# A three-layer graph network on one core: the order of the first seventy microseconds

## The chip, the cores and the metric

The kernel runs on one core of a Trainium2 chip. Its time is what one execution takes on the device, in microseconds; several executions are timed and their median is given. One more execution is recorded by the hardware profiler, and all rows of a trace come from that one.

Each core has TensorE (matmuls and transposes), VectorE (in the trace DVE), ScalarE (ACT), GpSimd (POOL) and SyncE (SP, which here only issues transfers). Every engine works off its own list in order, and the lists are tied by semaphores.

## The reference

```python
edge_index = stack([src, dst])                  # 20000 edges, 1250 nodes, 512 features, fp32
h = maximum(layernorm(x), 0)                    # first norm, with relu
x = x + L0(h, edge_index, ...)
h = maximum(layernorm(x), 0)
x = x + L1(h, src, dst, ...)                    # three graph convolutions

# L0 (GATv2 attention and a feed-forward net)
h1 = layer_norm(h, ln1_g, ln1_b)                # second norm
xl, xr = h1 @ Wl, h1 @ Wr                       # 8 heads of 64
e = sum over c of leaky_relu(xl[src] + xr[dst], 0.2) * att
alpha = softmax of e over the edges of one dst
h = h + segment_sum(alpha * xl[src], dst) + gat_bias
h = h + gelu(layer_norm(h, ln2_g, ln2_b) @ W1 + b1) @ W2 + b2
# L1: three times layer_norm, * 1/sqrt(out_degree), @ W[i], sum over edges, * 1/sqrt(in_degree), relu
```

## The kernel before

The 1250 nodes are ten blocks of 128 rows (NB = 10, the last one short). For the norms the blocks go in five groups of two (NG2 = 5, TWO = 2). `x_in` holds the rows as loaded and later the twice normed ones, `state` the once normed ones.

**What the first stage does.** Four things run side by side up to some 220 us.

*The norms.* For a group g, VectorE takes the statistics of the rows of x (`x_average(0, g)`: one bn_stats per block, L1340, and one bn_aggr, L1343), ScalarE the root (`x_root(0, g)`, L957), VectorE the reciprocal and the shift (`x_rows_scale(0, g)`, L1349 and L1351), and ScalarE writes the normed rows with relu to `state` (`x_norm(0, g)`, L964). The same four steps follow for the second norm, with nth = 1: VectorE reads `state` for its statistics, and ScalarE writes `x_in` (L966). The order is a pipeline over t: `norm_x(first, end)` on VectorE does average(0, t), rows_scale(0, t−1), average(1, t−2), rows_scale(1, t−3), and ScalarE's loop from L972 does root(0, t), norm(0, t−1), root(1, t−2), norm(1, t−3).

*The projections* of the twice normed rows by Wl, Wr and the folded attention weights. TensorE and ScalarE each have a generator, `projections()` (L609 and L922), cut into the same 90 steps: one for the transposes of block 0, then nine per block (the transposes of the next block, four matmuls for Wl, four for Wr with the attention product behind the last; the last block has eight). `advance(projecting, n)` runs n of them. On ScalarE a step is mostly empty: the first of a block moves the turned rows out of PSUM (`evict_block`, L913), the fifth copies the left rows (L942, to a tile), the last one the right rows (L942, to `xr_lo`) and three small things. TensorE may not write a block's right (or left) rows into their bank before ScalarE has copied those of the block before (`rows_kept`, L627). An fp32 matmul shows as two instructions in the trace.

*The sort of the edges by target*, in two radix passes on VectorE: `count_digits` compares (L1246) and scans (L1248), TensorE sums the counts (`digit_sums`), `start_digits` reads them (L1259), `place_edges` makes each edge's place (L1270, L1272 and the halving adds L1278, the first of them on 16 x 160 elements). Then `hot_batches` writes one-hot rows in batches (L1312 to L1322), and TensorE's `pick` multiplies them (L650, 32 instructions per batch, nine batches). The first pass is radix LOW = 32, the second HIGH = 40.

*The folds*: `fold_weights` multiplies Wl and then Wr by the attention vector (L1358) and sums per head (L1360). It needs the weights and the vector in SBUF.

**Where the lists meet.** TensorE advances 24 steps (COUNT_STEPS), does `digit_sums(LOW)`, advances 24 (LOW_STEPS), does pick(0), advances 18 (HIGH_STEPS), `digit_sums(HIGH)`, the other 24, and pick(1). On ScalarE the five x_norm(1, g) are followed by 6, 18, 3, 3 and 0 steps (NORM_STEPS), and then comes the rest. On VectorE: the digits of the edges (to L1411), norm_x(0, 4), the two att operations (L1414, L1416), both folds, norm_x(4, 5), count_digits(LOW), norm_x(5, 8), start_digits, place_edges(LOW), the hot batches. SyncE issues edges, x of groups 0 to 3, the zeros for two scatter tables, five rows of vectors, att, Wl, x of group 4, Wr and two biases, in this order (L437 to L459).

Behind this stage come the gathers of 352 tiles of source rows by GpSimd with the attention scores (to some 600 us), the feed-forward net, and the three convolutions. The change leaves them as they are; they start when the second pass has given the source of every edge.

Of the kernel before, what the change touches and what calls it, by code (L numbers as in the profile page):

```python
# [52 lines left out]
def build(nc, ins, out):  # L53
# [43 lines left out]
    with ExitStack() as ctx:  # L97
# [128 lines left out]
        pick_col = [rings.take(BATCH // QUARTET, max(NC, EJ), QUARTET, dt=FP16) for _ in range(2)]  # L226
        products = [ranked[:, side * KC * D:(side + 1) * KC * D] for side in range(2)]
# [112 lines left out]
        NORM_STEPS = [6, 18, 3, 3, 0]  # L340
        COUNT_STEPS, LOW_STEPS, HIGH_STEPS = 24, 24, 18
# [56 lines left out]
        x_averaged, x_rooted, x_scaled = ([count(f"{name}_{nth}") for nth in ("first", "second")] for name in ("x_averaged", "x_rooted", "x_scaled"))  # L398
# [37 lines left out]
        def sync(s):  # L436
# [7 lines left out]
            for t in range(NG2 - 1):  # L444
                load_x(t)
# [3 lines left out]
            for name, at, n in vector_rows:  # L449
                src = ins[name]  # L450
                if len(src.shape) == 2:
                    src = src.rearrange("l d -> (l d)")
                s.dma_start(columns_in[at:at + n, :], src.rearrange("(k p) -> k p", p=P)).then_inc(d_vectors, 16)
            s.dma_start(att_linear, spread(ins["L0_gnn_att"].rearrange("h c -> (h c)"))).then_inc(d_wide, 16)
            s.dma_start(w_left, w_view(ins["L0_gnn_Wl"])).then_inc(d_w[0], 16)
            load_x(NG2 - 1)
            s.dma_start(w_right, w_view(ins["L0_gnn_Wr"])).then_inc(d_w[1], 16)
# [445 lines left out]
        def scalar(a):  # L903
# [68 lines left out]
            for t in range(NG2 + 3):  # L972
                if t < NG2:
                    x_root(0, t)
                if 0 <= t - 1 < NG2:
                    x_norm(0, t - 1)
                if 0 <= t - 2 < NG2:
                    x_root(1, t - 2)
                if 0 <= t - 3 < NG2:
                    x_norm(1, t - 3)  # L980
                    if t == 3:
                        a.wait_ge(vectors_turned.sem, 1)
                        a.activation(columns[:, :], bank[:, 7, 0:VECTORS], ACT.Copy).then_inc(*columns_ready.up())
                        a.wait_ge(*columns_ready.now())
                    advance(projecting, NORM_STEPS[t - 3])
# [233 lines left out]
        def vector(v):  # L1219
# [20 lines left out]

            def count_digits(radix):

                s3 = by_digit(running, radix)
                v.wait_ge((digits_high if radix == HIGH else digits_low).sem, 1)
                v.wait_ge(*vo.now())
                v.tensor_tensor(by_digit(match, radix), over(digit[R0, :], 1, radix), digits[R0, 0:radix, :], ALU.is_equal).then_inc(*vo.up())  # L1246
# [14 lines left out]
            def place_edges(radix, by):  # L1261
# [7 lines left out]
                else:  # L1269
                    v.tensor_tensor(r3, by_digit(running, radix), over(base_of[R0, 0:radix], 2, EJ), ALU.add).then_inc(*vo.up())  # L1270
                    v.wait_ge(*vo.now())
                    v.tensor_tensor(r3, r3, by_digit(match, radix), ALU.mult).then_inc(*vo.up())  # L1272
                n = radix
                while n > 1:
# [3 lines left out]
                    v.tensor_tensor(out_ap, r3[:, 0:half, :], r3[:, n - half:n, :], ALU.add).then_inc(*vo.up())  # L1278
                    n -= half
# [54 lines left out]
            def x_average(nth, g):  # L1334
                for b in range(g * TWO, (g + 1) * TWO):
                    if nth:
                        v.wait_ge(once_normed.sem, b + 1)
                    elif b % TWO == 0:
                        v.wait_ge(d_x[g], 32)
                    v.bn_stats(stat[:, b, :], (state if nth else x_in)[:, b, :]).then_inc(*vo.up())  # L1340
                v.wait_ge(*vo.now())
                for b in range(g * TWO, (g + 1) * TWO):
                    ins_ = v.bn_aggr(x_moments[:, nth, b, :], stat[:, b, :])  # L1343
                ins_.then_inc(*x_averaged[nth].up())

            def x_rows_scale(nth, g):
# [4 lines left out]
                v.scalar_tensor_tensor(x_shift[:, nth, blocks], x_moments[:, nth, blocks, 0], -1.0, x_scale[:, nth, blocks], ALU.mult, ALU.mult).then_inc(*x_scaled[nth].up())  # L1351
# [9 lines left out]

            def norm_x(first, end):

                for t in range(first, end):
                    if t < NG2:
                        x_average(0, t)
                    if 0 <= t - 1 < NG2:
# [521 lines left out]
```

## Time and profile before

| | us |
|---|---|
| median of 3 runs | 1290.12 |
| lowest, highest | 1282.86, 1291.03 |
| the profiled execution | 1294.07 |
| its span in the trace | 1291.8 |
| busy in the span: TensorE, VectorE, ScalarE, GpSimd | 1075.5, 1029.4, 676.3, 444.2 |

The shares of busy time (TensorE 83%, VectorE 80%) are means over stages with different limits. What an edit in the first stage is worth can only be read there: which engine's list ends a wait last, and at what time the next stage can start. In the rows, a time in square brackets behind an instruction is the idle time of its engine just before it and what ended that. Groups of equal instructions are merged into one row, with "x" and their number; the second column is then the time of them all.

### The profile page before, as it was taken

The numbers are of one execution on the slowest core, as the hardware profiler recorded it, in microseconds if no ns is written. First come the engines' busy times: TensorE is split into PE (matmuls) and PEld (weight loads), VectorE is DVE, ScalarE is ACT, GpSimd is POOL, SyncE is SP. The second block draws the span as 40 slices with busy tenths as digits, with TensorE's granted clock in tenths as the row PEclk, the third lists the DMA queues.
The fourth block names the chain that finished last, engine by engine and source line by source line (L and its number), as shares of the span: only waits on it lengthen the run. The fifth ranks groups of instructions, "written<-read, shape, count | busy, mean of one in ns | idle before, by whom it ended". The sixth has DMA issues, their size and how long they took to land.

```text
span 1291.8 us, 15548 instructions
## 1 busy us (share of the span) xinstructions
PE 1075.5 (83%) x4827; PEld 800.3 (62%) x4847; DVE 1029.4 (80%) x1458; ACT 676.3 (52%) x1257; POOL 444.2 (34%) x412
## 2 busy tenths in 40 slices
PE   3979988565565656289999999699999999999998
PEld 2578456354454545145555555399888888889896
DVE  8999998587777778899999999875776778583934
ACT  4601300365555556278888888767655674342420
POOL 2071072655656555267778665000002100000000
PEclk9989889667767677589999999899999999999999
DMA  5000001655656556256666677400001202001002
GB/s 185 34 10 14 25 10 27 190 160 158 174 153 174 155 158 145 68 159 190 184 195 191 191 197 177 145 2 17 9 1 34 64 3 78 4 1 41 1 1 81
DMA packets 43434, 122.81 MB, mean 95 GB/s; under 512 B 7839, under 2 KB 8627, under 8 KB 43353
## 3 DMA queue, kind: packets, MB, share of 16 engines
q0 software_dynamic: 29184, 93.81, 27.1%
q1 hardware_dynamic: 14168, 27.98, 6.5%
q8 instruction: 44, 0.72, 0.2%
q14 instruction: 38, 0.30, 0.1%
HBM read 116.13 MB, written 5.59 MB: 94 GB/s over the span
## 4 chain that ended last, share of the span: by engine, by line
PE 56%; DVE 16%; ACT 13%; issue 7%; another core or an unknown queue 6%; DMA 1%; SPq 1%; ACTq 1%; DVEq 0%
PE bank L847 10%; PE bank L807 8%; PE bank L793 8%; PE bank L755 7%; PE bank L863 7%; PE bank L650 5%; PE bank L766 5%; PE bank L701 3%; ACT bank L1006 3%; ACT counts L1033 2%; ACT arena L991 2%; ACT hot_t L996 2%; ACT hot L920 1%; DVE counts L1248 1%
## 5 line engine op out<-in xcount | busy, mean ns | idle before, releaser
L568 POOL DMA_INDIRECT arena<-left_table,arena x352 | 364.7, 1036 | 241.1 <-issue 104.5
L701 PE MATMUL bank<-xr_hi,hot_t 128*128 x176 | 103.1, 586 | 120.6 <-ACT bank L1006 85.7
L755 PE MATMUL bank<-arena,hot 128*128 128x512 f32 x352 | 177.4, 620 | 4.0 <-DVE den_parts L1583 4.0
L1493 DVE SCALAR_TENSOR_TENSOR arena<-bank,arena 128x1024 f32<-128x1024 f32 x88 | 107.7, 1224 | 72.8 <-remote 37.0
L847 PE MATMUL bank<-counts_r,ns 128*128 128x512 f32 (+2 forms) x720 | 137.1, 349 | 0.0
L847 PEld LDWEIGHTS bank<-counts_r,ns 128*128 128x128 f32 x720 | 125.6, 188 | 10.4
L1033 ACT ACTIVATE counts<-bank 128x1280 f32 x88 | 108.9, 1237 | 39.9 <-issue 20.2
L701 PEld LDWEIGHTS bank<-xr_hi,hot_t 128*128 128x128 f32 x176 | 46.4, 264 | 130.8 <-issue 124.6
L991 ACT ACTIVATE arena<-bank,minus_own 128x512 f32<-128x512 f32 x44 | 30.2, 687 | 171.8 <-PE bank L691 86.3
L766 PE MATMUL bank<-arena 128*128 128x512 bf16 (+1 forms) x508 | 109.4, 347 | 6.6 <-DVE arena L1591 3.9
L1495 DVE TENSOR_REDUCE arena<-arena 128x16 f32<-128x1024 f32 x88 | 107.4, 1220 | 3.0
L1579 DVE TENSOR_TENSOR arena<-arena 128x1024 f32<-128x1024 f32 x88 | 107.1, 1217 | 0.0
L560 POOL DMA_INDIRECT moved<-counts x32 | 57.6, 1801 | 131.2 <-DVE counts L1297 61.7
L756 PE MATMUL bank<-den_parts,hot 128*128 128x18 f32 x176 | 101.9, 579 | 0.0
L650 PE MATMUL bank<-arena 125*125 125x160 f16 (+1 forms) x576 | 89.8, 332 | 13.1 <-DVE arena L1316 13.1
L650 PEld LDWEIGHTS bank<-arena 125*125 125x125 f16 (+1 forms) x576 | 74.8, 157 | 28.3 <-DVE arena L1316 16.6
L1006 ACT ACTIVATE bank<-arena 128x1024 f32<-128x1024 f32 x88 | 89.6, 1019 | 4.1 <-PE bank L717 2.7
L701 PE MATMUL bank<-xr_lo,hot_t 128*128 x176 | 91.0, 517 | 0.0
L1591 DVE TENSOR_SCALAR arena<-arena 128x1280 bf16<-128x1280 f16 x176 | 90.1, 553 | 0.8 <-PE bank L766 0.5
L766 PEld LDWEIGHTS bank<-arena 128*128 128x128 bf16 x528 | 52.5, 117 | 58.7 <-issue 16.7
L592 POOL CAST counts_r<-counts 128x1280 fp32r<-128x1280 f32 x10 | 13.1, 1313 | 203.9 <-issue 172.4
L629 PE MATMUL bank<-arena 128*128 128x512 f32 x160 | 77.7, 639 | 0.8 <-ACT arena L913 0.8
(248 smaller groups left out, 2203.0 us busy)
## 6 DMA issues: line engine op xcount, KB each, us to landing
arena<-left_table,arena POOLq DMA_INDIRECT x352
arena<-in_x_dram SPq DMA_DIRECT2D x18, 256.0 KB, 4.7
arena<-in_L_gnn_W_dram SPq DMA_DIRECT2D x8, 512.0 KB
arena<-in_L_gnn_W_dram SPq DMA_DIRECT2D x2, 1536.0 KB, 10.7
arena<-in_L_gnn_W_dram SPq DMA_DIRECT2D x3, 1024.0 KB, 5.4
left_table<-arena SPq DMA_DIRECT2D x10, 260.0 KB, 2.0
out_dram<-state SPq DMA_DIRECT2D x9, 256.0 KB
arena<-in_L_gnn_Wl_dram SPq DMA_DIRECT2D x1, 1024.0 KB, 9.9
```

The source lines that it names most:

```text
L568: g.indirect_dma_start(out=gathered[n % DEPTH][:, i, :], out_offset=None, in_=left_table, in_offset=bass.IndirectOffsetOnAxis(ap=src_of[:, ...
L650: ins_ = t.matmul(bank[0:out_rows, psum, 0:width], rows[R0, at[0], 0:out_rows, at[1]], pick_col[n % 2][R0, at[0], 0:width, at[1]], start=( ...
L701: ins_ = t.matmul(bank[:, 2 * (n % ZRING) + i, :], mine, part[:, bass.ds(at, 1), :].rearrange("p b n -> p (b n)"), start=False, stop=(part ...
L755: t.matmul(bank[:, psum, :], as_float(hot[c % 4]), w[:, i, :], start=(i == 0), stop=(i == 1))
L766: ins_ = t.matmul(flat[:, COUNT_AT + at:COUNT_AT + end], low_hot[n // 2 % 2][:, :, c % QUARTET], code_hot[c % 4][:, at:end], start=(c == 0 ...
L793: ins_ = t.matmul(bank[:, s, 0:cols], a[:, k, :], b[:, k, 0:cols], start=(i == 0), stop=(i == len(terms) - 1))
L847: ins_ = t.matmul(bank[:, SUM_BANKS[part][k], 0:n], lhs, rhs, start=(s == 0 and half == 0), stop=(s == NB - 1 and half == 1))
L1006: a.activation(bank[:, at:at + 2, :], gathered[n % DEPTH][:, :, 0:D], ACT.Copy).then_inc(*seeded.up())
L1033: a.activation(counts[:, :, bass.ds(at * P, P)], flat[:, COUNT_AT:COUNT_AT + NP].rearrange("p (b n) -> p b n", n=P), ACT.Copy).then_inc(*c ...
L1493: v.scalar_tensor_tensor(y, bank[:, at:at + 2, :], 0.0, over(att_relu, 1, 2), ALU.max, ALU.mult).then_inc(*rows_weighted.up())
L1495: v.tensor_reduce(sc, y.rearrange("p i (h c) -> p (i h) c", c=C), AX.X, ALU.add).then_inc(*pair_scored.up())
L1579: v.tensor_tensor(w.rearrange("p i (h c) -> p i h c", c=C), gathered[s][:, :, 0:D].rearrange("p i (h c) -> p i h c", c=C), over(weights[:, ...
```

## The change

1. **Second statistics.** VectorE's bn_stats and bn_aggr on `state` go. ScalarE's first norm (Relu) now also gives its sum over the row (`accum_out`), VectorE turns that into minus the mean (`x_mean`), and ScalarE makes a Square of the once normed rows with that as bias, whose sum is 512 times the variance (`x_spread`, results thrown away in `squares`). The root scales by 1/512.
2. **Order of the norms.** Both engines get a list written out by hand. On ScalarE the steps of the projections stand between the norms of single groups.
3. **VectorE.** The att operations come before the norms. `count_digits` is split: the comparison (`match_digits`) comes earlier. The folds stand between the steps of the first groups. The last steps of groups 3 and 4 stand inside `place_edges(LOW)`: behind its add, its multiplication and its first halving add.
4. **TensorE** advances 22, 24 and 20 steps in place of 24, 24 and 18.
5. **Loads.** SyncE issues x of groups 0 and 1, Wl, Wr, x of groups 2 to 4, and then the zeros. ScalarE's own queue issues att and the five rows of vectors, ahead of everything else it does.

```diff
+        squares = [ranked[:, LOW * EJ + i * D:LOW * EJ + (i + 1) * D] for i in range(TWO)]
...
-        NORM_STEPS = [6, 18, 3, 3, 0]
-        COUNT_STEPS, LOW_STEPS, HIGH_STEPS = 24, 24, 18
+        COUNT_STEPS, LOW_STEPS, HIGH_STEPS = 22, 24, 20
...
-            for t in range(NG2 - 1):
+            load_x(0)
+            load_x(1)
+            s.dma_start(w_left, w_view(ins["L0_gnn_Wl"])).then_inc(d_w[0], 16)
+            s.dma_start(w_right, w_view(ins["L0_gnn_Wr"])).then_inc(d_w[1], 16)
+            for t in range(2, NG2):
                 load_x(t)
...
             def x_root(nth, g):
                 blocks = slice(g * TWO, (g + 1) * TWO)
-                a.wait_ge(x_averaged[nth].sem, g + 1)
-                a.activation(x_scale[:, nth, blocks], x_moments[:, nth, blocks, 1], ACT.Sqrt, bias=eps[:, :]).then_inc(*x_rooted[nth].up())
+                if nth:
+                    a.wait_ge(x_squared.sem, (g + 1) * TWO)
+                else:
+                    a.wait_ge(x_averaged.sem, g + 1)
+                a.activation(x_scale[:, nth, blocks], x_moments[:, nth, blocks, 1], ACT.Sqrt, bias=eps[:, :], scale=1.0 / D if nth else 1.0).then_inc(*x_rooted[nth].up())
+
+            def x_spread(g):
+
+                a.wait_ge(x_centred.sem, g + 1)
+                if g:
+                    a.wait_ge(x_squared.sem, g * TWO)
+                for b in range(g * TWO, (g + 1) * TWO):
+                    a.activation(squares[b % TWO], state[:, b, :], ACT.Square, bias=x_moments[:, 1, b, 0:1], accum_out=x_moments[:, 1, b, 1:2]).then_inc(*x_squared.up())
...
-                        a.activation(state[:, b, :], x_in[:, b, :], ACT.Relu, bias=shift, scale=scale).then_inc(*once_normed.up())
+                        a.activation(state[:, b, :], x_in[:, b, :], ACT.Relu, bias=shift, scale=scale, accum_out=x_moments[:, 1, b, 0:1]).then_inc(*once_normed.up())
...
+            a.dma_start(att_linear, spread(ins["L0_gnn_att"].rearrange("h c -> (h c)"))).then_inc(d_wide, 16)
+            for name, at, n in vector_rows:
+                a.dma_start(columns_in[at:at + n, :], ins[name].rearrange("(k p) -> k p", p=P)).then_inc(d_vectors, 16)
...
+            x_root(0, 0)
+            x_norm(0, 0)
+            x_root(0, 1)
+            x_spread(0)
+            x_root(1, 0)
+            a.wait_ge(vectors_turned.sem, 1)
+            a.activation(columns[:, :], bank[:, 7, 0:VECTORS], ACT.Copy).then_inc(*columns_ready.up())
+            a.wait_ge(*columns_ready.now())
+            x_norm(1, 0)
+            advance(projecting, 1)
+            x_norm(0, 1)
+            advance(projecting, 1)
+            x_spread(1)
+            x_root(1, 1)
+            x_norm(1, 1)
+            advance(projecting, 4)
+            x_root(0, 2)
+            advance(projecting, 3)
+            x_norm(0, 2)
+            advance(projecting, 9)
+            x_spread(2)
+            x_root(1, 2)
+            x_root(0, 3)
+            x_norm(1, 2)
+            x_norm(0, 3)
+            advance(projecting, 4)
+            x_root(0, 4)
+            x_spread(3)
+            x_root(1, 3)
+            x_norm(0, 4)
+            advance(projecting, 5)
+            x_norm(1, 3)
+            x_spread(4)
+            x_root(1, 4)
+            x_norm(1, 4)
             advance(projecting, STEPS)
...
                     v.tensor_tensor(r3, by_digit(running, radix), over(base_of[R0, 0:radix], 2, EJ), ALU.add).then_inc(*vo.up())
+                    beside[0]()
                     v.wait_ge(*vo.now())
                     v.tensor_tensor(r3, r3, by_digit(match, radix), ALU.mult).then_inc(*vo.up())
+                    beside[1]()
...
                     v.tensor_tensor(out_ap, r3[:, 0:half, :], r3[:, n - half:n, :], ALU.add).then_inc(*vo.up())
+                    if n == radix and beside:
+                        beside[2]()
...
+            def x_mean(g):
+
+                own = x_moments[:, 1, g * TWO:(g + 1) * TWO, 0]
+                v.wait_ge(once_normed.sem, (g + 1) * TWO)
+                v.tensor_scalar(own, own, -1.0 / D, None, ALU.mult).then_inc(*x_centred.up())
...
-            norm_x(0, 4)
             v.wait_ge(d_wide, 16)
             v.tensor_scalar(att_relu, att_linear, 1.0 - SLOPE, None, ALU.mult).then_inc(*vo.up())
             v.wait_ge(*vo.now())
             v.tensor_scalar(att_linear, att_linear, SLOPE, None, ALU.mult).then_inc(*att_split.up())
+            x_average(0)
+            x_rows_scale(0, 0)
+            x_average(1)
+            x_mean(0)
+            x_rows_scale(0, 1)
+            match_digits(LOW)
+            x_rows_scale(1, 0)
             fold_weights(0, w_left)
+            x_mean(1)
             fold_weights(1, w_right)
-            norm_x(4, 5)
+            x_rows_scale(1, 1)
+            x_average(2)
+            x_rows_scale(0, 2)
             count_digits(LOW)
-            norm_x(5, NG2 + 3)
+            x_mean(2)
+            x_average(3)
+            x_rows_scale(1, 2)
+            x_rows_scale(0, 3)
+            x_average(4)
             start_digits(LOW).then_inc(*vo.up())
-            place_edges(LOW, EJ)
+            place_edges(LOW, EJ, {0: lambda: (x_mean(3), x_rows_scale(0, 4)), 1: lambda: x_rows_scale(1, 3), 2: lambda: (x_mean(4), x_rows_scale(1, 4))})
```

## Rows read from the trace of the kernel before

**Rows 1.** Chain of waits from the start: start us, us, what.

```profile
8.93 9.93 DMA arena<-in_L_gnn_Wl_dram
...
61.66 2.84 DVE arena L1278
```

**Rows 2.** Stages: busy us (instructions) per engine, PEclk granted clock, DMA share, GB/s.

```profile
4.00:8.00 4.00, 0.00 (x0) 0.00 (x0) 2.88 (x9) 0.30 (x1) 3.84 (x10) 1.00 0.94 285
...
51.00:69.00 18.00, 17.57 (x62) 9.09 (x60) 17.66 (x13) 11.24 (x31) 0.00 (x0) 1.00 0.10 37
...
139.00:142.00 3.00, 3.00 (x6) 1.45 (x6) 2.29 (x12) 0.00 (x0) 0.00 (x0) 0.50 0.03 8
```

**Rows 3.** VectorE in order of time: start us, us, line, operation, shapes, count.

```profile
7.67 1.29 DVE L1340 BATCH_NORM_STATS2 stat<-arena 128x6 f32<-128x512 f32 x2 [0.64 <-DMA arena<-in_x_dram]
...
11.13 1.28 DVE L1340 BATCH_NORM_STATS2 stat<-state 128x6 f32<-128x512 f32 x2
...
12.60 1.25 DVE L1340 BATCH_NORM_STATS2 stat<-arena 128x6 f32<-128x512 f32 x2
...
18.88 2.30 DVE L1358 TENSOR_TENSOR arena<-arena 128x2048 f32<-128x2048 f32 x1 [1.98 <-DMA arena<-in_L_gnn_Wl_dram]
...
47.62 1.40 DVE L1340 BATCH_NORM_STATS2 stat<-state 128x6 f32<-128x512 f32 x2
...
49.21 0.13 DVE L1349 RECIPROCAL counts<-counts 128x2 f32<-128x2 f32 x1
...
50.11 0.17 DVE L1349 RECIPROCAL counts<-counts 128x2 f32<-128x2 f32 x1 [0.56 <-ACT counts L957]
...
68.87 1.19 DVE L1312 TENSOR_TENSOR arena<-counts 125x2000 f16<-125x2000 f16 x1
```

**Rows 4.** ScalarE in order of time, the same columns.

```profile
0.80 1.28 ACT L970 ACT_TABLE_LOAD   x1 [0.80 <-PEq L1879]
...
7.07 0.30 ACT L957 ACTIVATE counts<-counts,eps 128x2 f32<-128x2 f32 x1 [4.77 <-DVE counts L1343]
...
49.97 1.51 ACT L966 ACTIVATE arena<-state,counts 128x512 f32<-128x512 f32 x2
51.38 0.58 ACT L942 ACTIVATE xr_lo<-bank 128x512 f32<-128x512 f32 x1
```

**Rows 5.** TensorE in order of time, the same columns.

```profile
33.27 8.27 PE L629 MATMUL bank<-arena 128*128 128x512 f32 x16
...
50.77 0.64 PE L606 MATMUL bank<-ident,arena 128*128 128x128 f32 x4
51.25 7.03 PE L629 MATMUL bank<-arena 128*128 128x512 f32 x16
58.12 0.96 PE L639 MATMUL bank<-arena 128*128 128x16 f32 x8
58.92 0.64 PE L606 MATMUL bank<-ident,arena 128*128 128x128 f32 x4
...
74.87 5.42 PE L650 MATMUL bank<-arena 125*125 125x160 f16 x35 [6.30 <-DVE arena L1316]
...
118.36 6.19 PE L629 MATMUL bank<-arena 128*128 128x512 f32 x14
...
137.68 0.41 PE L657 MATMUL bank<-counts,ones 125*125 125x40 f32 x2 [2.84 <-DVE counts L1254]
...
139.15 9.14 PE L629 MATMUL bank<-arena 128*128 128x512 f32 x14
```

**Rows 6.** ScalarE's groups by line: busy us, mean ns of one | idle before.

```profile
L991 ACT ACTIVATE arena<-bank,minus_own 128x512 f32<-128x512 f32 x44 | 30.2, 687 | 171.8 <-PE bank L691 86.3 <-remote 75.5 <-issue 10.0
...
L970 ACT ACTIVATE deviation<-eps 128x1 f32<-128x1 f32 x1 | 0.2, 203 | 0.0
```

**Rows 7.** Transfers by line: KB each, median us from issue to landing.

```profile
arena<-in_x_dram SPq DMA_DIRECT2D x18, 256.0 KB, 4.7
...
arena<-in_L_gnn_Wl_dram SPq DMA_DIRECT2D x1, 1024.0 KB, 9.9
```

More of the change, by code:

```diff
@@ L396, in build @@
         hot_once, hot_src, batch_hot, picked = count("hot_once"), count("hot_src"), count("batch_hot"), count("picked")
-        x_averaged, x_rooted, x_scaled = ([count(f"{name}_{nth}") for nth in ("first", "second")] for name in ("x_averaged", "x_rooted", "x_scaled"))
+        x_rooted, x_scaled = ([count(f"{name}_{nth}") for nth in ("first", "second")] for name in ("x_rooted", "x_scaled"))
+        x_averaged, x_centred, x_squared = count("x_averaged"), count("x_centred"), count("x_squared")
         once_normed = count("once_normed")
@@ L448, in sync @@
                 s.dma_start(table.rearrange("(p c) w -> p (c w)", p=n), back[0:n, 0:table.shape[0] // n, :].rearrange("p c w -> p (c w)")).then_inc(d_zeros, 16)
[L449 to L457, printed above, removed]
             s.dma_start(gat_bias, spread(ins["L0_gnn_gat_bias"])).then_inc(d_bias, 16)
@@ L971, in scalar @@
             projecting = projections()
[L972 to L985, printed above, removed]
+            x_root(0, 0)
[33 more added lines that the diff above has]
+            x_norm(1, 4)
             advance(projecting, STEPS)
@@ L1239, in by_digit, with match_digits @@
                 return ap[R0, 0:radix * EJ].rearrange("p (k j) -> p k j", j=EJ)
-            def count_digits(radix):
-                s3 = by_digit(running, radix)
+            def match_digits(radix):
                 v.wait_ge((digits_high if radix == HIGH else digits_low).sem, 1)
@@ L1246, in count_digits @@
                 v.tensor_tensor(by_digit(match, radix), over(digit[R0, :], 1, radix), digits[R0, 0:radix, :], ALU.is_equal).then_inc(*vo.up())
+            def count_digits(radix):
+                s3 = by_digit(running, radix)
                 v.wait_ge(*vo.now())
@@ L1259, in start_digits, with place_edges @@
                 return v.scalar_tensor_tensor(base_of[R0, 0:radix], bank[R0, 6, 0:radix], -1.0, shifted[R0, 0:radix], ALU.add, ALU.subtract)
-            def place_edges(radix, by):
+            def place_edges(radix, by, beside={}):
                 r3 = by_digit(ranked, radix)
@@ L1332, in beside_pick, with x_average @@
                 v.tensor_tensor(state[:, blocks, :], state[:, blocks, :], over(gat_bias, 1, end - first), ALU.add).then_inc(*biased.up(end - first))
-            def x_average(nth, g):
+            def x_average(g):
                 for b in range(g * TWO, (g + 1) * TWO):
-                    if nth:
-                        v.wait_ge(once_normed.sem, b + 1)
-                    elif b % TWO == 0:
+                    if b % TWO == 0:
                         v.wait_ge(d_x[g], 32)
-                    v.bn_stats(stat[:, b, :], (state if nth else x_in)[:, b, :]).then_inc(*vo.up())
+                    v.bn_stats(stat[:, b, :], x_in[:, b, :]).then_inc(*vo.up())
                 v.wait_ge(*vo.now())
                 for b in range(g * TWO, (g + 1) * TWO):
-                    ins_ = v.bn_aggr(x_moments[:, nth, b, :], stat[:, b, :])
-                ins_.then_inc(*x_averaged[nth].up())
+                    ins_ = v.bn_aggr(x_moments[:, 0, b, :], stat[:, b, :])
+                ins_.then_inc(*x_averaged.up())
+            def x_mean(g):
+                own = x_moments[:, 1, g * TWO:(g + 1) * TWO, 0]
+                v.wait_ge(once_normed.sem, (g + 1) * TWO)
+                v.tensor_scalar(own, own, -1.0 / D, None, ALU.mult).then_inc(*x_centred.up())
             def x_rows_scale(nth, g):
@@ L1350, in x_rows_scale @@
                 v.wait_ge(*vo.now())
-                v.scalar_tensor_tensor(x_shift[:, nth, blocks], x_moments[:, nth, blocks, 0], -1.0, x_scale[:, nth, blocks], ALU.mult, ALU.mult).then_inc(*x_scaled[nth].up())
+                if nth:
+                    v.wait_ge(x_centred.sem, g + 1)
+                v.scalar_tensor_tensor(x_shift[:, nth, blocks], x_moments[:, nth, blocks, 0], 1.0 if nth else -1.0, x_scale[:, nth, blocks], ALU.mult, ALU.mult).then_inc(*x_scaled[nth].up())
             def fold_weights(side, w):
@@ L1360, in fold_weights @@
                 v.tensor_reduce(wa[:, :, side, :], p.rearrange("p (k h c) -> p k h c", k=KC, c=C), AX.X, ALU.add).then_inc(*att_folded.up())
[L1362 to L1367, printed above, removed]
-                        x_rows_scale(0, t - 1)
-                    if 0 <= t - 2 < NG2:
-                        x_average(1, t - 2)
-                    if 0 <= t - 3 < NG2:
-                        x_rows_scale(1, t - 3)
             def pad_blocks():
@@ L1436, in vector @@
             v.tensor_copy(digit[R0, :], digit_i[R0, :]).then_inc(*vo.up())
+            match_digits(HIGH)
             count_digits(HIGH)
```

## The prediction

> **What bounds the kernel now.** I read first the chain of waits from the start [rows 1]. Up to 8.93 us it is the issue queue of SyncE, then the load of Wl (9.93 us); VectorE's two folds, the second norm, some projection and VectorE's placing of the edges follow, up to the first one-hot pick on TensorE at 74.87. The stages [rows 2] say the same: from 51 to 69 us VectorE is busy 17.66 of 18 us, ScalarE only 11.24. So until 74.87 VectorE's list is the limit and TensorE has its 48 projection steps done 6.30 us too early, at 68.57 [rows 5]. After that picks and one-hot batches alternate. The later stages (gathers, messages, feed-forward, convolutions) aren't touched; they start when the keys are there, so what matters is how far the start of the first pick batch, **74.87**, moves.
>
> **VectorE's list, part by part** [rows 3]. Its landmark in both kernels: the end of the first of place_edges' halving adds, now 61.66 + 2.84 = 64.50 [rows 1].
> - Removed: five second statistics (bn_stats twice, bn_aggr twice). The first runs from 11.13 to the next group's start at 12.60, 1.47 us, three more alike, the last from 47.62 to 49.21, 1.59: together 7.5 us.
> - Waits that go: 1.98 us for Wl before the fold (18.88), 0.64 for the second pair of x (7.67), 0.56 for the last root (50.11): 3.2 us. Wl goes with that because the queue now issues it behind four x loads. The bytes before its end are then 156 (edges) + 256 (att, 128x512 like one block of x, from ScalarE's queue) + 1024 + 1024 KB; the first x pair was there at 5.44 with 668 KB, and the rest, 1.8 MB at the 285 GB/s of 4 to 8 us, takes 6.4 us: there at some 11.8, and Wr 3.7 us later [rows 2, 7]. VectorE wants Wl at 14.1.
> - Added: five x_mean on 128x2. The nearest row is a reciprocal on 128x2 (50.11), 0.17 long with some of it overlapped: 0.6 us in all, bounds 0.3 and 0.9.
> - Moved: match_digits, both folds and the two att operations: same lengths, other place. The pair for (1,4) goes behind the landmark, −0.3.
> - The start: att's 256 KB come before x, which at 285 GB/s sets the first pair 0.9 us back, to 6.3; the att operations fill 5.3 to 6.2. Together nothing.
> - New waits, from laying the three engines' new lists beside each other with these durations. x_rows_scale(0,0) now directly follows its own average and waits out the root, 0.3. x_mean(0) waits for two Relus, 0.45. x_mean(1) waits for ScalarE, which has norm(1,0), one block's evictions and norm(0,1) beside the fold, 0.65. x_rows_scale(0,2) waits because its root stands behind norm(1,1) and an eviction, 0.9. x_rows_scale(1,2) waits for Square and root behind the scan, 0.45. Sum 2.8; bounds 1.5 (accumulating costs nothing) and 4.
>
> Landmark after: 64.5 − 7.5 − 3.2 + 0.6 − 0.3 + 2.8 = **56.9**, 7.6 us earlier. SyncE's queue loses six small issues, and ScalarE's gets them: it has nothing but one little Sqrt to do before 7.07, with 4.77 us idle just before [rows 4], so an issue could take 0.7 us and be hidden; if it were dearer, the first root would slip and the landmark with it. The zeros for the scatter are written later, behind the x loads; they are wanted only behind the places at 68.87.
>
> **Prices on ScalarE** [rows 4, 6]. No accumulated ACTIVATE is in the trace. Below, it costs nothing more; above, a second little instruction as long as the shortest one, 0.20 us (L970). I take 0.2 as nearest. A Square with one pointer operand: nearest L991, 0.69; two in a row with the sums 1.6 us (bounds 1.3 and 2.0). **But its list is in order, and that is where I see the gain end.** Before, ScalarE never waited for anything behind place_edges: it copied block 2's right rows (L942) at 51.38. Now it reaches that copy (step 28, as `advance` has then given 1+1+4+3+9+4+5 = 27) only behind x_norm(1,4). That waits for x_rows_scale(1,4), that for the Squares of group 4, and these for x_mean(4), which VectorE issues behind the landmark. From the landmark: x_mean 0.12, Squares 1.6, root 0.28, reciprocal and shift 0.3, norm 1.5, copy 0.6, handovers 0.1 = 4.5: rows kept at **61.4** instead of 51.96.
>
> **TensorE then** [rows 5]. Side 1 of block 3 can't overwrite the bank before that copy (rows_kept ≥ 6). After it stand side 1 of block 3 (8 of a block's 16 instructions in 7.03, 3.44 with their overlap), its att product (58.12 to 58.92: 0.80) and one whole block (50.77 to 58.92: 8.15): 12.4 us, ending at 73.8 at full clock. Before the copy it has some 5.5 us of nothing to do. The trace shows what follows such a gap: after 2.84 us of idleness the same 14 matmuls took 9.14 us, at a granted clock of 0.50 (the 1.2 GHz level), against 6.19 (the 2.4 GHz level), +2.95 [rows 2, 5]; earlier a block's 16 took 8.27 instead of 7.03, +1.24. I take 2.3, nearer to the longer gap: **76.1**. The 46 steps are needed before pick(0), so the first batch starts there and not at VectorE's own time.
>
> VectorE itself: landmark 56.9, a wait of 2.0 for Squares and root in x_rows_scale(1,4), 0.3, the other adds and the quotient 4.4, then 6.0 up to the first batch (68.87 to 74.87) = 69.6. It is 6.5 us ahead of TensorE: the roles are exchanged. From the landmark TensorE needs 16.9 us at full clock, VectorE 12.7, so an earlier landmark doesn't turn this round.
>
> **Picks and behind.** With VectorE a batch ahead, TensorE no longer waits a little before every other batch; I take −0.5, bounds 0 and −1. The two steps that move behind the pick (a transpose and one matmul pair: 0.64 + 0.86 less overlap = 1.34) lie under the scan of HIGH: TensorE was ready 2.84 us before digit_counts there [rows 5], it is still by 1.5. If that cover were gone they would cost 1.34. The order of match_digits(HIGH) is unchanged.
>
> **Sum**: 76.1 − 74.87 − 0.5 = **+0.7 us**. On the profiled execution (1294.07, span 1291.8) that is 1294.8. This execution stands 3.95 above the median of the runs, 1290.12; against the median I forecast 1290.8, rounded **1291**. Some 7.6 us are gained on VectorE and all of them lost in the order of ScalarE's list.
>
> **Rivals.**
> (a) *VectorE sets the start of the pick*: the first batch at 69.6, −5.3, time 1284.8. For it: in the profile VectorE is the limit and TensorE waits 6.30 us. It needs the copy of step 28 by 55.2, before x_mean(4) can even start. That contradicts the two lists; I give it 0.12, for a clock or a landmark much kinder than worked out.
> (b) *Slower: Square is not in the table loaded with Sqrt.* ScalarE alternates Square and Sqrt five times, and each change would be an ACT_TABLE_LOAD of 1.28 us [rows 4]. The place that decides is behind the landmark: one load before the Squares, one before the root, +2.6 on the way to the copy. Of the eight before it (10.3 us), the 5.8 us (worked out as the waits above) in which ScalarE waits for the scan hide about half: +5. Time 1290.8 + 7.6 = 1298.4. Against it: in the first 69 us Sqrt, Relu, Identity and Copy alternate with one single load, the one at 0.80. I give it 0.06. The Trainium skill (ScalarE: Activation LUTs, Table sets: the hidden batching unit) names relu, copy, identity and abs as fillers of every set, square not, so by its list Square could need a switch; it puts one with its drain at about 2.66 us, by which (b) would cost about twice as much (an estimate from that page). No row here has a Square.
> (c) *Slower: the weights come late*, VectorE waits for Wr as it did for Wl, and the landmark slips by 2 to 4 us: 1294. It decides once Wr lands after 18.9; I count on 15.4. Chance 0.04.
> The forecast's own case (TensorE late, within −1.5 and +3): 0.78.
>
> **Range and chances.** Bounds of the sum: full clock −2.3, accumulation free −1.5 to −0.8, upper wait and price bounds +2. The runs themselves lie 7.3 below to 0.9 above their median, the profiled one 3.95 above. 1281 to 1297 takes in (a) and the run's spread. About 1% (13 us) is what a measurement can tell from no change: faster by more than that only in (a) with a low run, 0.06; slower only in (b), 0.04; within 0.90.
>
> **What would show it.** Right: one L1278 add ending near 57, ScalarE's L942 for block 2's right rows near 61, TensorE idle over 4 us before it and at half clock after, L650 starting near 76 with VectorE's L1316 done long before. Each accumulated activation followed by an instruction of about 0.2. Wrong: L650 released by VectorE (then (a)), an ACT_TABLE_LOAD between Square and Sqrt (b), a wait of the second fold for Wr (c), or VectorE's landmark off by over 2 us, with the wait list above at fault.

## The result and the profile after

| | before | after |
|---|---|---|
| median of 18 runs, us | 1290.16 | 1294.23 |
| lowest, highest | 1279.99, 1295.44 | 1289.48, 1300.15 |
| ratio after to before, with its 95% interval | | 1.0041 (1.0023 to 1.0058) |
| the profiled execution, its span | 1294.07, 1291.8 | 1294.23, 1292.1 |
| first pick batch starts | 74.87 | 79.61 |
| first gather starts | 220.94 | 225.47 |

The change costs 4.1 us by the medians, 3.0 to 7.5 by the interval: within 1%, inside the range, on the slower side of the forecast. The two profiled spans hardly differ, but that is chance: the profiled execution of before stands 3.9 above its median and that of after stands on its own. What single executions show well is the first stage: equal instructions in it come at nearly equal times in every trace (the one kernel below that was traced twice differs by 0.5 us up to the first gather). The first gather, which opens the stage that the change doesn't touch, starts **4.53 us later**, and that is the loss.

First VectorE's start (start us, us, line, operation, shapes, count; in brackets the idle time before and what ended it), to be laid beside [rows 3]:

```profile
6.17 1.15 DVE L1438 TENSOR_SCALAR counts<-counts 125x160 int32<-125x160 int32 x1 [2.54 <-DMA counts<-in_dst_dram]
7.24 1.28 DVE L1439 CAST counts<-counts 125x160 f16<-125x160 int32 x1
8.44 1.31 DVE L1440 CAST counts<-counts 125x160 f16<-125x160 int32 x1
9.78 0.24 DVE L1442 CAST counts<-counts 125x160 bf16<-125x160 int32 x1
...
10.74 1.28 DVE L1375 BATCH_NORM_STATS2 stat<-arena 128x6 f32<-128x512 f32 x2
...
58.12 2.82 DVE L1313 TENSOR_TENSOR arena<-arena 125x2560 f32<-125x2560 f32 x1
60.85 0.16 DVE L1385 TENSOR_SCALAR counts<-counts 128x2 f32<-128x2 f32 x1
62.93 0.17 DVE L1390 RECIPROCAL counts<-counts 128x2 f32<-128x2 f32 x1 [1.92 <-ACT counts L956]
```

The same start in the kernel before:

```profile
4.19 0.36 DVE L1407 TENSOR_SCALAR counts<-counts 125x160 int32<-125x160 int32 x1 [0.56 <-DMA counts<-in_dst_dram]
4.48 0.32 DVE L1408 CAST counts<-counts 125x160 f16<-125x160 int32 x1
4.71 0.22 DVE L1409 CAST counts<-counts 125x160 f16<-125x160 int32 x1
...
5.47 1.28 DVE L1340 BATCH_NORM_STATS2 stat<-arena 128x6 f32<-128x512 f32 x2 [0.22 <-DMA arena<-in_x_dram]
```

The edges are there at 6.17, in the kernel before at 4.19. The three digit operations on them take 1.15, 1.28 and 1.31 us; before they took 0.36, 0.32 and 0.22. So the first statistics start at 10.74 instead of 5.47. The landmark, the end of the first halving add, is at 58.12 + 2.82 = 60.94, 3.6 us before that of before [rows 1].

In the same stretch, GpSimd's list in the kernel after:

```profile
5.63 1.60 POOL L546 IOTA counts<- 128x704 f16 x1
7.18 1.24 POOL L547 IOTA arena<- 128x1280 f16 x1
8.38 1.27 POOL L548 IOTA counts<- 128x1280 bf16 x1
```

These end at 7.23, 8.42 and 9.65; VectorE's three slow operations end at 7.32, 8.52 and 9.75, each a tenth of a microsecond behind an iota. In the kernel before the same iotas ran from 5.72 to 9.66, when the digit operations were done (at 5.25).

Now ScalarE behind the landmark, to be laid beside [rows 4]:

```profile
61.05 0.72 ACT L964 ACTIVATE arena<-state,counts 128x512 f32<-128x512 f32 x1 [1.29 <-DVE counts L1385]
61.68 0.19 ACT L964 ACTIVATION_READ_ACCUMULATOR arena<-state,counts 128x1 f32 x1
...
63.33 1.52 ACT L973 ACTIVATE arena<-state,counts 128x512 f32<-128x512 f32 x2 [0.43 <-DVE counts L1394]
64.75 0.57 ACT L938 ACTIVATE xr_lo<-bank 128x512 f32<-128x512 f32 x1
```

The copy of block 2's right rows starts at 64.75; it was at 51.38. Each accumulated sum shows as an instruction of its own, of 0.19 us. TensorE, to be laid beside [rows 5]:

```profile
56.37 3.67 PE L625 MATMUL bank<-arena 128*128 128x512 f32 x8 [1.24 <-ACT arena L938]
65.47 5.34 PE L625 MATMUL bank<-arena 128*128 128x512 f32 x8 [5.43 <-ACT xr_lo L938]
70.65 0.96 PE L635 MATMUL bank<-arena 128*128 128x16 f32 x8
...
71.93 7.03 PE L625 MATMUL bank<-arena 128*128 128x512 f32 x16
78.80 0.96 PE L635 MATMUL bank<-arena 128*128 128x16 f32 x8
79.61 4.71 PE L646 MATMUL bank<-arena 125*125 125x160 f16 x31
```

TensorE stands still for 5.43 us, released by exactly that copy; the eight matmuls behind the gap take 5.34 us where the eight before it took 3.67. And L646, the pick, which is L650 in the kernel before, has no idle time before it at all: in the kernel before it had 6.30 us and waited for VectorE. The stages behind the gap (busy us per engine, then the granted clock, DMA share, GB/s):

```profile
65.00:67.00 2.00, 1.53 (x2) 0.84 (x3) 1.86 (x5) 1.94 (x8) 0.00 (x0) 0.61 0.05 18
67.00:69.00 2.00, 2.00 (x4) 0.74 (x3) 1.94 (x5) 1.25 (x4) 0.35 (x1) 0.54 0.30 115
69.00:71.00 2.00, 2.00 (x9) 1.04 (x8) 2.00 (x2) 0.15 (x1) 1.70 (x2) 1.00 0.06 1
```

The granted clock is near its lower level (0.5, 1.2 GHz) until 69 us and full (2.4 GHz) from then on.

### The profile page after: what moved, and what is told of

Its sections match the earlier page's. It is cut to its first block, busy times and chain, and to the rows that moved or that the text cites. A ratio compares the mean times of both kernels' runs of the same rounds, so it can differ in the third digit from the quotient of the medians.

```text
span 1292.1 us, 15572 instructions
## 1 busy us (share of the span) xinstructions
PE 1081.9 (84%) x4827; PEld 803.3 (62%) x4847; DVE 1024.2 (79%) x1443; ACT 685.1 (53%) x1287; POOL 425.7 (33%) x412
## 4 chain that ended last, share of the span: by engine, by line
PE 62%; DVE 15%; ACT 12%; another core or an unknown queue 6%; issue 5%; ACTq 0%; DMA 0%; DVEq 0%; SPq 0%
PE bank L843 10%; PE bank L751 9%; PE bank L803 8%; PE bank L789 8%; PE bank L859 7%; PE bank L762 6%; PE bank L646 5%; PE bank L697 5%; ACT bank L1037 3%; ACT counts L1064 2%; DVE counts L1281 2%; ACT arena L1022 2%; ACT hot_t L1027 1%; ACT hot L916 1%
## 5 line engine op out<-in xcount | busy, mean ns | idle before, releaser
L564 POOL DMA_INDIRECT arena<-left_table,arena x352 | 348.8, 991 | 253.1 <-issue 95.7
L697 PE MATMUL bank<-xr_hi,hot_t 128*128 x176 | 106.1, 603 | 109.3 <-ACT bank L1037 80.3
L556 POOL DMA_INDIRECT moved<-counts x32 | 55.0, 1719 | 138.3 <-DVE counts L1334 70.2
L646 PE MATMUL bank<-arena 125*125 125x160 f16 (+1 forms) x576 | 89.7, 332 | 8.1 <-DVE arena L1353 8.1
L646 PEld LDWEIGHTS bank<-arena 125*125 125x125 f16 (+1 forms) x576 | 75.0, 156 | 22.3 <-DVE arena L1353 10.7
```

What stands on the lines that cost most here:

```text
L564: g.indirect_dma_start(out=gathered[n % DEPTH][:, i, :], out_offset=None, in_=left_table, in_offset=bass.IndirectOffsetOnAxis(ap=src_of[:, ...
L646: ins_ = t.matmul(bank[0:out_rows, psum, 0:width], rows[R0, at[0], 0:out_rows, at[1]], pick_col[n % 2][R0, at[0], 0:width, at[1]], start=( ...
L697: ins_ = t.matmul(bank[:, 2 * (n % ZRING) + i, :], mine, part[:, bass.ds(at, 1), :].rearrange("p b n -> p (b n)"), start=False, stop=(part ...
```

## The experiments

Experiments 1 to 4 ran on a chip on which the kernel before takes 1290 us, experiments 5 to 9 and the second run of experiment 2 on two others, on which it takes 1221; a ratio is always to runs of before on the same chip. Times up to the first gather are compared across chips with the trace of before, which was taken where it takes 1290. How far that can be trusted shows in experiment 2, whose kernel was traced on a chip of either kind: its first gather starts at 220.39 and 220.91. Experiments 4 to 7 have one execution each and are read by their traces alone. Line numbers differ by a few from version to version.

**1. The copies before the last Squares.** Only ScalarE's list is changed.

```diff
             x_norm(0, 4)
-            advance(projecting, 5)
-            x_norm(1, 3)
+            advance(projecting, 11)
             x_spread(4)
             x_root(1, 4)
+            x_norm(1, 3)
             x_norm(1, 4)
```

> The kernel after, with one change in ScalarE's list: behind x_norm(0,4) it advances 11 steps instead of 5 (so both copies of block 2 and the left copy of block 3 come before the Squares of group 4), and x_norm(1,3) moves behind x_root(1,4). Theory A (the order of ScalarE's list holds TensorE back): the copy of block 2's right rows near 57 instead of 64.8, TensorE without its gap of 5.4 us and done with 46 steps near 72.5, the first pick batch at 73.6 instead of 79.6, now released by VectorE; time 6 us below the kernel after, 1 to 2 below the one before. Rival B (TensorE is late because of the clock or the number of steps, not of the copy): the first batch stays within 2 us of 79.6.

Measured: TensorE's rows are

```profile
56.37 7.11 PE L625 MATMUL bank<-arena 128*128 128x512 f32 x16 [1.28 <-ACT arena L938]
63.31 0.96 PE L635 MATMUL bank<-arena 128*128 128x16 f32 x8
...
71.46 0.96 PE L635 MATMUL bank<-arena 128*128 128x16 f32 x8
73.55 9.61 PE L646 MATMUL bank<-arena 125*125 125x160 f16 x64 [1.13 <-DVE arena L1353]
```

One run of 16 matmuls stands where a gap was, and the pick starts at 73.55, released by VectorE. The median is 1287.17, the ratio to the kernel before 0.9984 (0.9966 to 1.0003), which can't be told from no change; the first gather starts at 219.66, 5.8 us earlier than in the kernel after. From the first statistics on VectorE's list is the same to a hundredth of a microsecond (10.73, and the halving add at 58.11). So the order of ScalarE's list alone moves the pick by 6 us. It is the term that the prediction named.

**2. The loads back on SyncE's queue.** ScalarE issues nothing; the att operations stand before the first fold.

```diff
             load_x(1)
+            s.dma_start(att_linear, ...).then_inc(d_wide, 16)
+            for name, at, n in vector_rows:
+                s.dma_start(columns_in[at:at + n, :], ...).then_inc(d_vectors, 16)
             s.dma_start(w_left, w_view(ins["L0_gnn_Wl"])).then_inc(d_w[0], 16)
...
             x_rows_scale(1, 0)
+            v.wait_ge(d_wide, 16)          # and the two att operations, which stood before x_average(0)
```

> The kernel after, but att and the five rows of vectors are issued by SyncE again, behind the x of groups 0 and 1, and VectorE's two att operations stand just before the first fold. Theory A (the 4.4 us that VectorE's list starts late come from att's bytes ahead of the edges, 2.0 us, and from the digit operations then falling on GpSimd's iotas, 2.8 us): edges there at 4.2, the three digit operations 0.2 to 0.4 us each as before, first statistics at 5.5 instead of 10.7, end of the first halving add at 56.5 instead of 60.9, first pick batch at 75.2 instead of 79.6, still released by TensorE. Rival B (the digit operations are slow whatever the loads do): statistics at 8 or later, first batch at 77.5 or later.

Measured: edges at 4.37, and from there

```profile
4.37 0.33 DVE L1438 TENSOR_SCALAR counts<-counts 125x160 int32<-125x160 int32 x1 [0.74 <-DMA counts<-in_dst_dram]
4.62 0.22 DVE L1439 CAST counts<-counts 125x160 f16<-125x160 int32 x1
...
5.79 1.29 DVE L1375 BATCH_NORM_STATS2 stat<-arena 128x6 f32<-128x512 f32 x2 [0.51 <-DMA arena<-in_x_dram]
```

The landmark is at 53.34 + 2.82 = 56.16 (the prediction had 56.9), the pick starts at 74.55, still behind TensorE's gap of 5.43 us, and the first gather at 220.39. Theory A holds. Timed again:

> e1 again, now timed. By its trace the first gather starts 0.6 us before that of the kernel before, so theory A expects the same time as before (ratio 0.9995) and rival B, by which something behind the gathers' start costs or gives, more than 3 us away from it.

The ratio is 1.0004 (0.9994 to 1.0015), with the first gather at 220.91. With the start mended no gain or loss of the rest of the change can be told apart from nothing, which agrees with the prediction's sum (+0.7).

**3. Both.**

The edits of experiments 1 and 2 together.

> Both of the edits: loads of att and vectors by SyncE, att operations before the first fold, and ScalarE's copies first. Theory A: VectorE's landmark (first halving add) at 56.5, first pick batch at 69.2, released by VectorE, 5.7 us earlier than in the kernel before and 10.4 earlier than in the one after; time 5 to 6 us below before (ratio 0.9955). Rival B (another wait takes their place, for instance TensorE's step count, and ends behind VectorE): first batch at 72 or later, time as before.

Median 1284.80, ratio 0.9954 (0.9933 to 0.9976): below both. Against experiment 2 the intervals are clear of each other, against experiment 1 they overlap, and there the pick shows the difference. The landmark comes at 53.38 + 2.82 = 56.20, the pick at 70.02 (expected 69.2), released by VectorE. The miss of 0.8 us is in VectorE's wait for the last root, 3.12 us where experiment 1 had 1.92: the Squares of group 4 stand behind ScalarE's left copy of block 3, which waited 2.64 us for TensorE. And TensorE was slow there: its 16 matmuls took 8.80 us in place of 7.11, at a granted clock of 0.60 and 0.55 between 52 and 56 us.

**4. Why the digit operations are slow.**

```diff
+            g.wait_ge(vo.sem, DIGITS_BY_VECTOR + 4)      # VectorE's four digit operations
             g.iota(iota_four, ...)
```

> The kernel after; GpSimd's last three iotas wait for VectorE's four digit operations. Theory A (the digit operations are held up by the iotas running beside them on GpSimd): edges still late at 6.2, but the three digit operations 0.2 to 0.4 us each instead of 1.15 to 1.31, the first statistics at 8.0 instead of 10.7, first pick batch at 76.9. Rival B (they are slow because of the transfers that land in SBUF then): 1.1 to 1.3 us each as before, statistics at 10.7.

VectorE and GpSimd, as measured:

```profile
6.14 0.24 DVE L1439 TENSOR_SCALAR counts<-counts 125x160 int32<-125x160 int32 x1 [2.52 <-DMA counts<-in_dst_dram]
6.30 0.24 DVE L1440 CAST counts<-counts 125x160 f16<-125x160 int32 x1
...
6.88 0.42 DVE L1446 TENSOR_SCALAR arena<-arena 128x512 f32<-128x512 f32 x1
7.34 1.65 DVE L1448 TENSOR_SCALAR arena<-arena 128x512 f32<-128x512 f32 x1
```

```profile
7.04 1.67 POOL L547 IOTA counts<- 128x704 f16 x1 [1.36 <-DVE counts L1443]
8.67 1.42 POOL L548 IOTA arena<- 128x1280 f16 x1
```

The edges are as late as before, and each digit operation takes 0.24 us. So it is GpSimd's iotas and not the transfers. The expectation missed what comes next: the statistics start at 8.91, not 8.0, because now the second att operation (7.34) falls on the iota that began at 7.04 and takes 1.65 us instead of 0.43. Its predecessor, already running when the iota began, took 0.42. The pick starts at 77.83, the first gather at 223.67, 1.8 us earlier than in the kernel after.

**5. What makes the edges late.** On ScalarE's queue the five rows of vectors go first, att last.

```diff
-            a.dma_start(att_linear, ...).then_inc(d_wide, 16)
             for name, at, n in vector_rows:
                 a.dma_start(columns_in[at:at + n, :], ...).then_inc(d_vectors, 16)
+            a.dma_start(att_linear, ...).then_inc(d_wide, 16)
```

> The kernel after; on ScalarE's queue the five rows of vectors are issued before att, which is then issued at about 2.9 us instead of 0.8. Theory A (att's 256 KB in front delay the edges): edges at 4.2 to 4.6 instead of 6.1; att lands later, at 6 to 8. Rival B (the vectors' small transfers, or a second queue as such, delay them): edges stay at 6 or later.

The edges are there at 4.23, so it is att's 256 KB, issued first, at 0.80, that stood in their way; the vectors, issued there now, don't. Att itself, issued at 2.77, now lands at 10.64, later than I expected:

```profile
4.23 0.33 DVE L1438 TENSOR_SCALAR counts<-counts 125x160 int32<-125x160 int32 x1 [0.60 <-DMA counts<-in_dst_dram]
...
10.64 0.43 DVE L1444 TENSOR_SCALAR arena<-arena 128x512 f32<-128x512 f32 x1 [5.40 <-DMA arena<-in_L_gnn_att_dram]
```

As VectorE's list has att before the first statistics, it waits 5.40 us there and the pick starts at 80.25, worse than in the kernel after. So with att on ScalarE's queue, first or last, the early place of its operations costs.

**6. The loads alone, in the kernel before.** Att and the vectors are issued by ScalarE's queue first, all else as before.

```diff
-            for name, at, n in vector_rows:              # SyncE, behind the zeros
-                ...
-            s.dma_start(att_linear, ...).then_inc(d_wide, 16)
...
+            a.dma_start(att_linear, ...).then_inc(d_wide, 16)      # ScalarE, first thing
+            for name, at, n in vector_rows:
+                a.dma_start(columns_in[at:at + n, :], ...).then_inc(d_vectors, 16)
```

> The kernel before; only att and the five rows of vectors are issued from ScalarE's queue, ahead of everything else it does, as the change does it; all the rest, Wl's place behind the zeros too, as before. Theory A: this part alone costs time. Edges at 6.2 instead of 4.2, digit operations over 1.1 us each, first statistics near 9.9 instead of 5.5; of these 4.4 us the waits for x (0.64) and for Wl (1.98) take back 2.6, so the halving add ends near 66.4 instead of 64.5 and the first pick batch starts near 76.7 instead of 74.9. Rival B (the late start is an effect of the reordered x and weights): statistics at 5.5 to 6.5, first batch at 75.

Edges at 6.14, the three operations 1.17, 1.28 and 1.31 us, the first statistics at 9.93, the pick at 76.07 and the first gather at 222.58, 1.64 us later than before. The expected 76.7 was a little high. So this part costs by itself. The statistics are 4.5 us late and the pick only 1.2, since waits that the kernel before has anyway shrink: 1.98 us for Wl, 0.64 for x, and most of the 0.56 for the last root.

**7. The statistics alone, in the kernel before.** The Squares stand just before the second root, x_mean stands in the place of the second x_average.

```diff
             def x_root(nth, g):
+                if nth:
+                    a.wait_ge(x_centred.sem, g + 1)
...
+                    for b in range(g * TWO, (g + 1) * TWO):
+                        a.activation(squares[b % TWO], state[:, b, :], ACT.Square, bias=..., accum_out=...).then_inc(*x_squared.up())
+                    a.wait_ge(x_squared.sem, (g + 1) * TWO)
...
             def x_average(nth, g):
+                if nth:
...
+                    v.tensor_scalar(own, own, -1.0 / D, None, ALU.mult).then_inc(*x_centred.up())
+                    return
```

> The kernel before; only the second statistics are changed: x_mean on VectorE in the place of the second x_average, and the Squares on ScalarE just before the second root, in the old pipeline order, with the old loads and steps. Theory A (what VectorE saves is taken back by ScalarE's list, whose Squares and roots follow each other behind the copy of step 24): of VectorE's 7.5 us, 3 fall into the wait for Wl, which grows from 2.0 to about 5; behind the scan VectorE waits for ScalarE for 6 us or more, start_digits at 54 to 55 instead of 50.4, first pick batch at 79 instead of 74.9, still released by VectorE. Rival B (fewer VectorE operations pay by themselves): start_digits at 46 to 48, first batch at 71 to 73.

VectorE's rows behind the scan:

```profile
48.22 0.17 DVE L1348 TENSOR_SCALAR counts<-counts 128x2 f32<-128x2 f32 x1 [3.61 <-ACT state L974]
49.95 0.17 DVE L1364 RECIPROCAL counts<-counts 128x2 f32<-128x2 f32 x1 [1.57 <-ACT counts L967]
53.10 0.17 DVE L1364 RECIPROCAL counts<-counts 128x2 f32<-128x2 f32 x1 [2.79 <-ACT counts L967]
```

It waits 8.0 us for ScalarE where it waited 0.56 before. The pick starts at 77.88, the first gather at 223.95, 3.0 us later than before. Theory A holds in kind; the wait for Wl is 2.63 and not 5, since VectorE had lost 1.56 us to a root already at 14.84. Taking work from VectorE does not pay by itself here, in the old order of the lists.

**8. The last scale beside the adds.** Experiment 3, and x_rows_scale(1, 4) behind the last halving add.

```diff
-            place_edges(LOW, EJ, {..., 2: lambda: (x_mean(4), x_rows_scale(1, 4))})
+            place_edges(LOW, EJ, {..., 2: lambda: x_mean(4), 3: lambda: x_rows_scale(1, 4)})      # 3: once half == 1
```

> e3 (loads by SyncE, ScalarE's copies first) and x_rows_scale(1,4) moved from behind the first halving add to behind the last one, so that the Squares and the root of group 4 run beside VectorE's adds. Theory A: VectorE's wait of 1.9 us there goes; the first pick batch moves from 69.2 to 67.5 to 68.3, where TensorE's 46 steps may end last; time 7 us below before (ratio 0.994). Rival B: TensorE or ScalarE is late by more, the first batch at 69 or later.

Median 1214.18 against 1221.04 of before on that chip, ratio **0.9947** (0.9934 to 0.9961). The pick starts at 67.19, with no idle time before it, so TensorE ends last again (VectorE had the first batch at 65.15 + 1.19 = 66.34); the first gather starts at 213.02, 7.9 us earlier than before. By the first gather this is the fastest version; by the ratio it can't be told from experiment 3 (0.9954).

**9. One copy too early: a miss.** Experiment 8, and ScalarE makes block 1's right copy before the Squares of group 2.

```diff
-            advance(projecting, 9)
+            advance(projecting, 10)
             x_spread(2)
...
             x_norm(0, 3)
-            advance(projecting, 4)
+            advance(projecting, 3)
```

> e9 with one more edit in ScalarE's list: 10 steps instead of 9 before x_spread(2), 3 instead of 4 behind x_norm(0,3), so that the copy of block 1's right rows no longer stands behind the Squares that wait for the scan. Theory A: TensorE's wait of 3.3 us before block 2's right side goes and its 46 steps are done near 62 instead of 67.2; the first batch is then released by VectorE at 66.4 (60.4 + 6.0), 0.8 us earlier than e9; ratio to before 0.994. Rival B (the copy now delays group 2's Squares, since it waits for TensorE): VectorE's chain 1 us or more later, first batch at 67.2 or later.

TensorE's next wait took the place of the one removed, and is longer:

```profile
44.38 0.63 PE L605 MATMUL bank<-ident,arena 128*128 128x128 f32 x4
51.31 9.98 PE L628 MATMUL bank<-arena 128*128 128x512 f32 x16 [6.29 <-ACT arena L941]
```

It comes to block 3 earlier, but the left copy of block 2 still stands behind the Squares of group 3, which wait for VectorE's x_mean(3) behind its add of 5.5 us. In experiment 8 block 3's matmuls started at the same time:

```profile
51.29 7.11 PE L628 MATMUL bank<-arena 128*128 128x512 f32 x16 [1.26 <-ACT arena L941]
```

So nothing is won, and what is lost is in the clock: the granted clock was 0.50 from 51 to 57 us, where experiment 8 had 1.00 from 51 to 55, and the 16 matmuls take 9.98 us. The pick starts at 70.09, 2.9 us later than in experiment 8; the ratio is 0.9965 (0.9951 to 0.9978). My expectation looked at one gate, a point where a list waits for another engine, and not at the next.

All versions side by side, against the kernel before:

| | first pick | first gather | gather against before | time against before by the ratio |
|---|---|---|---|---|
| after | 79.61 | 225.47 | +4.5 | +5.3 (+3.0 to +7.5) |
| loads by SyncE (second run) | 75.11 | 220.91 | 0.0 | +0.5 (−0.7 to +1.8) |
| copies first | 73.55 | 219.66 | −1.3 | −2.1 (−4.4 to +0.4) |
| both | 70.02 | 215.84 | −5.1 | −5.9 (−8.6 to −3.1) |
| both, late scale | 67.19 | 213.02 | −7.9 | −6.5 (−8.1 to −4.8) |
| one copy too early | 70.09 | 215.88 | −5.1 | −4.3 (−6.0 to −2.7) |

What the first gather gains or loses, the whole kernel does, within the intervals.

## Why the prediction was right, and where it was off

**The mechanism holds.** VectorE's list gains and TensorE decides, because ScalarE's copy of block 2's right rows stands behind x_norm(1,4). From the landmark to the end of that copy 4.4 us passed (4.5 forecast), and from there to the pick 14.3 (12.4 + 2.3 forecast). VectorE by itself would have had the pick at 73.55, as experiment 1 shows, with the landmark where it was; in the kernel after, VectorE has that batch ready at 73.51 (72.32 + 1.19, L1353). Rival (a) is refuted by L646's missing idle time. Rival (b) too: no table load stands between Square and Sqrt. The one load in the first 225 us is at 3.54. The filler list of the Trainium skill (ScalarE: Activation LUTs, Table sets: the hidden batching unit), which doesn't name square, was no warning here. Rival (c): the second fold didn't wait for Wr.

**The term that was mis-sized is the start**, "Together nothing" in the prediction's list. It measured +4.44 us: the first statistics at 10.74 where I had 6.3. I had reckoned 0.9 us for att's bytes, against x, but they stand before the edges too, where they cost 2.0 us, and VectorE's list waits for the edges first; and I hadn't asked what GpSimd does in the microseconds into which the digit operations slide (2.8 us more in the three of them). Experiments 2, 4, 5 and 6 show both halves. From the first statistics to the landmark it was 50.2 us against 50.6 forecast, so the rest of VectorE's list, the removed 7.5 us and the new waits included, came out right as a sum.

**The new waits**, forecast 0.3, 0.45, 0.65, 0.9 and 0.45, measured 0.36, 0.29, 0.71, 0.78 and 0.45: 2.6 us together against 2.8.

**The clock behind the gap**: 5.34 against 3.67 us for eight matmuls, +1.67, where I took 2.3; between the bounds of 1.24 and 2.95. My reason for 2.3, that a longer gap costs more, isn't borne out: 5.43 us of gap cost less than the 2.84 us in the kernel before. In experiment 3 eight matmuls behind a gap of 3.65 us took 3.67, no more than at full clock, and the 16 behind the next gap, of 2.81, took 8.80. That the value lay near was in part luck. The forecast also has no gap at block 2: there TensorE waited 3.24 us (48.61) and its eight matmuls took 5.24, which the later wait of 5.43 us hides.

**The picks**: from the first pick to the first gather the kernel after is 0.2 us shorter (4.74 against 4.53), I took 0.5. The two steps moved behind the pick are hidden: TensorE still waits 1.54 us for digit_counts of HIGH (1.5 forecast).

**The sum**: +0.7 forecast. With the start as measured (+4.4), the clock (−0.6), the rest of VectorE's list (−0.4), copy and handover to the matmuls (−0.1 and +0.2) and the picks (+0.3) it is +4.5, against 4.53 at the first gather and 4.1 by the medians. With the start mended, experiment 2 measured +0.5 for it (−0.7 to +1.8) by the ratio, −0.6 and 0.0 by the first gather; its pick, at 74.55 and 75.11, comes before the 76.1 of the forecast.

**By its own signs** the prediction is right on who waits for whom. One sign of being wrong that it had named came true: the landmark is 4.0 us off, over the 2 us that it allowed. It would have blamed the wait list, and the fault was the start. The result lies 3.4 us above the forecast by the medians, 3.8 by the first gather, past the +3 of the forecast's own case. That the time is inside 1281 to 1297 owes much to the width of that range, made for rival (a) and the spread of the runs: it had room for a missed term of 4.4 us, six times the sum itself.

## What to carry to other kernels

When work moves between engines with in-order lists, follow the one operation that a third engine needs and write down everything that now stands before it: here the list that got shorter wasn't the one that ended last. A load that is issued earlier pushes back what it overtakes; ask what waits for that, and what runs beside it once it is late. A gate that is opened for a waiting engine is worth only the way to its next gate, so look at both before moving a step.

## What the runs showed of the hardware

GpSimd's iotas held up VectorE's casts and tensor_scalar operations until the iota was over: 1.15 to 1.31 us in place of 0.22 to 0.36, each ending 0.1 us behind an iota. One that was already running when the iota began wasn't slowed (0.42 at 6.88 in experiment 4), the next one was (1.65 for 0.43, ending 0.3 behind the iota). Bn_stats beside the same iotas in the kernel before was not (1.29 at 7.67, 1.28 elsewhere). The Trainium skill (SBUF — State Buffer, Who interferes with whom) says that VectorE in its two-port modes, open to casts and tensor_scalar, and GpSimd share a pair of ports, and that whoever issues first holds it for the whole instruction; the traces agree.

An accumulated ACTIVATE is two instructions: the second (ACTIVATION_READ_ACCUMULATOR) takes 0.18 to 0.22 us, of which some 0.1 overlaps its neighbours (the next Square starts 0.09 behind it).

The kernel of experiment 2 took 1288.81 us on one chip (one execution) and 1220.75 on another, with the first gather at 220.39 and 220.91. The difference lies behind it: from 300 to 600 us the first trace shows a granted clock of 0.71 for TensorE and 154 GB/s of transfers, the second 0.81 and 187. Which of these is cause and which effect wasn't tried.
